# Expert rows weighted by ScalarE on the way out of PSUM and added onto y by an accumulating gather

## The reference, cut to what matters

```python
_, ys = jax.lax.scan(step, h0, xs)            # h = clip(bar_A * h + bar_B * x), y = sum(h * C) + x * D
ssm_out = jnp.swapaxes(ys, 0, 1)
flat = ssm_out.reshape(-1, d)
routing = jax.nn.softmax(flat @ Wr + br, axis=1)
top1_w = jnp.max(routing, axis=1)
top1_i = jnp.argmax(routing, axis=1)
hid = jax.nn.silu(jnp.einsum('nd,edf->enf', flat, up_w) + up_b[:, None, :])
all_out = jnp.einsum('enf,efd->end', hid, down_w) + down_b[:, None, :]
sel = jnp.take_along_axis(jnp.swapaxes(all_out, 0, 1), top1_i[:, None, None], axis=1)[:, 0, :]
moe_out = (sel * top1_w[:, None]).reshape(Bb, Ll, d)
out = ssm_out + moe_out
mu = jnp.mean(out, axis=-1, keepdims=True)
var = jnp.mean((out - mu) ** 2, axis=-1, keepdims=True)
return (out - mu) * jax.lax.rsqrt(var + EPS) * ln_w + ln_b
```

## Time and profile before

| | |
|---|---|
| median of 3 runs | 930.92 us (927.97 to 935.09) |
| the profiled execution | 928.69 us, its span 926.9 us |
| granted clock of PE, mean | 0.826 of full |
| indirect DMAs | 64 scatters, 64 gathers |
| weightings (L1080) | 64 |

### The profile page before, as it was taken

The page is one execution under the profiler, slowest core; times in us unless marked ns, Lnnn a source line. Parts: engine busy times, 40 slices in busy tenths (PEclk is TensorE's granted clock), DMA queues, the critical chain, the costliest instruction groups (busy, mean ns, idle before and its releaser), DMA issues.

```text
span 926.9 us, 14132 instructions
## 1 busy us (share of the span) xinstructions
PE 636.4 (69%) x4238; PEld 511.0 (55%) x4296; DVE 717.1 (77%) x1458; ACT 536.8 (58%) x988; POOL 565.2 (61%) x452
## 2 busy tenths in 40 slices
PE   3466658783799568964898289946985589358454
PEld 1244436671687448853777178825874388247333
DVE  3699898789979998799879997999879976431251
ACT  5373274664886659583958487647853484155222
POOL 0366547567874887478757876588648853541431
PEclk8566776996899779995999599967997599669766
DMA  3333445764367536663675447653665266316200
GB/s 101 117 136 114 137 141 166 257 215 166 115 229 244 199 110 202 210 179 115 209 252 166 159 138 258 210 185 114 217 220 189 84 215 199 114 56 197 74 7 23
DMA packets 82087, 149.31 MB, mean 161 GB/s; under 512 B 9404, under 2 KB 51144, under 8 KB 81992
## 3 DMA queue, kind: packets, MB, share of 16 engines
q1 hardware_dynamic: 69192, 135.13, 44.8%
q0 software_dynamic: 4096, 8.40, 2.8%
q10 hardware_dynamic: 8704, 4.72, 1.8%
HBM read 132.80 MB, written 15.40 MB: 160 GB/s over the span
## 4 chain that ended last, share of the span: by engine, by line
PE 30%; DVE 23%; ACT 17%; issue 16%; POOL 6%; DMA 5%; SPq 1%; ACTq 1%; another core or an unknown queue 0%; DVEq 0%; POOLq 0%
DVE state L1163 9%; PE psU L649 5%; ACT hid L800 4%; PE psD L552 4%; PE psT L663 4%; DVE psB L1154 3%; DMA weights<-in_w_pack 3%; PE psU L688 3%; PE psY L528 3%; ACT decay L761 3%; PE psU L689 2%; ACT x L820 2%; DVE bst L1097 2%; PE psU L577 1%; PE psB L522 1%
## 5 line engine op out<-in xcount | busy, mean ns | idle before, releaser
L1190 POOL TENSOR_TENSOR prod<-state,c_wide 128x1024 f32<-128x1024 f32 x128 | 308.8, 2419 | 151.7 <-DVE state L1163 132.1
L1154 DVE TENSOR_TENSOR psB<-dx,psB 128x512 f32<-128x512 f32 x256 | 166.7, 689 | 27.9 <-PE psB L522 12.1
L1163 DVE TENSOR_TENSOR_SCAN state<-decay,state,psB 128x512 f32<-128x512 f32 x128 | 163.8, 1280 | 14.0
L522 PE MATMUL psB<-parts,sel 128*128 128x512 bf16 x198 | 89.2, 464 | 122.7 <-DVE state L1163 121.0
L1163 DVE TENSOR_TENSOR_SCAN state<-decay,psB 128x512 f32<-128x512 f32 x128 | 155.1, 1212 | 3.8 <-ACT decay L761 3.8
L528 PE MATMUL psY<-ident,prod 128*128 128x128 f32 x1024 | 156.8, 308 | 0.7 <-POOL prod L1190 0.5
L761 ACT ACTIVATE decay<-delta,a_sb 128x1024 f32<-128x1024 f32 x128 | 142.0, 1142 | 15.1 <-DVE state L1163 7.3
L528 PEld LDWEIGHTS psY<-ident,prod 128*128 128x128 f32 x1024 | 139.2, 161 | 12.5 <-issue 8.1
L522 PEld LDWEIGHTS psB<-parts,sel 128*128 128x128 bf16 x256 | 25.8, 103 | 176.1 <-DVE state L1163 166.0
L800 ACT ACTIVATE hid<-psU,weights 128x128 f32<-128x128 f32 x352 | 99.3, 370 | 37.8 <-PE psU L649 32.5
L649 PE MATMUL psU<-yT_sorted,weights 128*128 128x128 f32 x704 | 95.5, 280 | 19.3 <-DVE hh L1134 8.0
(11 more groups left out here) (151 smaller groups left out, 1110.8 us busy)
## 6 DMA issues: line engine op xcount, KB each, us to landing
c_wide<-c_rows SPq DMA_DIRECT2D x128, 512.0 KB
weights<-in_w_pack SPq DMA_DIRECT2D x88, 514.0 KB, 4.1
xT_sb<-in_xT SPq DMA_DIRECT2D x8, 512.0 KB, 4.2
y_sorted<-rows_in SPq DMA_DIRECT2D x16, 256.0 KB, 3.1
xt<-in_x SPq DMA_DIRECT2D x8, 512.0 KB, 4.2
rows_out<-result SPq DMA_DIRECT2D x16, 256.0 KB, 4.3
out<-x ACTq DMA_DIRECT2D x16, 256.0 KB, 2.7
y_sorted<-rows_in SPq DMA_DIRECT2D x8, 192.0 KB, 3.9
```

Of the source, the lines that this page charges most:

```text
L522: pe.matmul(tokens(psB, c, h), sel[:, s, :], parts[:, c.n % 2, h * HALF:h * HALF + c.hw], start=True, stop=True).then_inc(b_ready, 1)
L1154: v.tensor_tensor(tokens(psB, c, h), dx[:, n % 2, h * HALF:h * HALF + c.hw], tokens(psB, c, h), ALU.mult).then_inc(inp_ready, 1)
L1163: v.tensor_tensor_scan(state[:, g % NSTATE, t0:t0 + c.hw], decay[:, g % NDECAY, t0:t0 + c.hw], tokens(psB, c, h), before, ALU.mult, ALU.ad ...
L1190: g_.tensor_tensor(prod[:, g % NPROD, w], state[:, g % NSTATE, w], c_wide[:, g % NC, w], ALU.mult).then_inc(prod_ready, 1)
```

## The change

The weight of a token travels with its row. ytok, y_sorted and rows_in get a 129th column. `router_pick` writes the weight into that column of ytok, so it has to run before `scatter` 0, which now waits for it; in the lists it stands in front of `slots`, and `router_exp` in front of decay 3. The scatter moves 129 numbers a row. `result` reads the weight from y_sorted as the scale of an Identity, so the rows that are stored are weighted already; `rows` now waits for all results of the chunk before. The gather no longer fills chosen_out: it is an indirect DMA that adds onto ytok (`compute_op=ALU.add`). `combine`, its semaphores, chosen_out and top_w are gone; `stats` h, 0 and `centre` read ytok, and `stats` h, 0 waits for the gathers. `y_copy` waits for `centre` of the chunk two before. rows_in is zeroed at the start in another shape. The five lists are written anew. The transposes out of ytok and y_sorted and the biases at the start take columns 0 to 127 (not shown). Of the five lists the new entries up to the marks are shown; `combine` stood in front of `scan` 4 and behind `scan` 7 on DVE, `x_shift` 1 between `prod` 4 and `gather` 5 on POOL.

```diff
 PE_ORDER = [
+    (0, "spread", 2, 0), (0, "spread", 2, 1), (0, "skip"), (-1, "logits"), (0, "spread", 3, 0), (0, "add", 0),
+    (0, "spread", 3, 1), (-1, "rank"), (0, "add", 1), (0, "spread", 4, 0), (0, "spread", 4, 1), (1, "bc"),
+    (0, "spread", 5, 0), (0, "spread", 5, 1), (0, "add", 2), (0, "add", 3), (0, "spread", 6, 0), (0, "spread", 6, 1),
+    (0, "spread", 7, 0), (0, "spread", 7, 1), (-2, "x_turn", 0), (-2, "x_rest", 0), (0, "add", 4),
+    (-2, "ff_up", 0, 0), (0, "spread", 8, 0), (-2, "ff_up", 0, 1), (0, "spread", 8, 1), (-2, "ff_up", 0, 2),
+    (0, "add", 5), (-2, "ff_up", 0, 3), (-2, "ff_up", 0, 4), (1, "b_turn"), (0, "spread", 9, 0), (0, "spread", 9, 1),
+    (-2, "ff_up", 0, 5), (-1, "sort_turn", 0), (0, "add", 6), (-1, "up", 0), (-1, "up", 1), (0, "spread", 10, 0),
+    (-1, "sort_turn", 1), (0, "spread", 10, 1), (-1, "down", 0), (-1, "up", 2), (-1, "down", 1), (0, "add", 7),
+    (0, "spread", 11, 0), (0, "spread", 11, 1), (-1, "down", 2), (-1, "sort_turn", 2), (-1, "up", 3),
+    (1, "b_spread", 0), (-2, "ff_down", 0), (0, "add", 8), (-2, "ff_part", 0, 0), (-2, "ff_part", 0, 1),
...
 ACT_ORDER = [
+    (-2, "silu", 8), (-2, "result", 8), (-2, "silu", 9), (-2, "silu", 10), (-2, "result", 9), (0, "decay", 0),
+    (-2, "result", 10), (-3, "norm", 1, 2), (0, "decay", 1), (-1, "y_copy"), (0, "decay", 2), (-1, "yT_copy"),
+    (1, "z_copy"), (-1, "router_exp"), (0, "decay", 3), (0, "decay", 4), (0, "decay", 5), (1, "softplus"),
+    (0, "decay", 6), (1, "bc_copy"), (0, "decay", 7), (-2, "norm", 0, 1), (0, "decay", 8), (-2, "x_high", 0),
...
 DVE_ORDER = [
+    (-2, "ff_mul", 0, 0), (-2, "ff_mul", 0, 1), (1, "b_max"), (-2, "ff_mul", 0, 2), (0, "scan", 9), (0, "scan", 10),
+    (1, "bc_low"), (-2, "affine", 1), (-2, "stats", 1, 1), (0, "scan", 11), (1, "bound", 0), (-2, "stats", 0, 2),
+    (0, "scan", 12), (0, "scan", 13), (1, "dx"), (1, "bound", 1), (-2, "ff_mul", 1, 0), (1, "over"),
+    (-2, "ff_mul", 1, 1), (-2, "ff_mul", 1, 2), (0, "scan", 14), (1, "flag"), (-2, "stats", 1, 2), (0, "scan", 15),
+    (1, "scan", 0), (1, "scan", 1), (1, "scan", 2), (0, "router_shift"), (1, "scan", 3), (0, "router_pick"),
+    (0, "slots"), (-1, "stats", 0, 0), (1, "scan", 4), (-1, "centre", 0), (1, "scan", 5), (1, "scan", 6),
+    (-1, "affine", 0), (-1, "stats", 0, 1), (2, "delta"), (1, "scan", 7), (-1, "stats", 1, 0), (-1, "centre", 1),
+    (1, "scan", 8),
 POOL_ORDER = [
+    (-1, "prod", 15), (-2, "x_shift", 1), (0, "prod", 0), (-2, "gather", 0), (0, "prod", 1), (-2, "gather", 1),
+    (-2, "gather", 2), (-2, "gather", 3), (0, "prod", 2), (0, "prod", 3), (-2, "gather", 4), (-2, "gather", 5),
+    (-2, "gather", 6), (-1, "scatter", 0), (-1, "scatter", 1), (-2, "rstd", 0, 0), (-1, "scatter", 2), (0, "prod", 4),
+    (-2, "gather", 7), (-1, "scatter", 3), (-2, "rstd", 0, 1), (-1, "scatter", 4), (-1, "scatter", 5),
+    (-1, "scatter", 6), (-1, "scatter", 7), (0, "prod", 5), (0, "prod", 6), (1, "bc_rest"), (0, "prod", 7),
+    (0, "prod", 8), (-2, "rstd", 1, 0), (0, "prod", 9), (1, "bound_input"), (-2, "rstd", 1, 1), (0, "prod", 10),
+    (-2, "rstd", 0, 2), (0, "prod", 11), (-1, "x_shift", 0), (0, "prod", 12), (0, "prod", 13), (0, "prod", 14),
+    (-2, "rstd", 1, 2),
 SP_ORDER = [
+    (-2, "c", 5), (-3, "weights", 1), (-3, "weights", 2), (-2, "c", 6), (-2, "c", 7), (-3, "rows"), (-2, "c", 8),
+    (-2, "c", 9), (-2, "c", 10), (-3, "weights", 3), (-2, "c", 11), (-3, "weights", 4), (-3, "weights", 5), (-3, "x"),
+    (-2, "c", 12), (-3, "weights", 6), (-2, "c", 13), (-3, "weights", 7), (-3, "weights", 8), (-3, "weights", 9),
+    (-1, "over"), (-2, "c", 14), (-3, "weights", 10), (-2, "c", 15), (-1, "c", 0), (-3, "store", 0), (0, "xT"),
+    (-1, "c", 1), (-3, "store", 1), (-3, "store", 2), (-1, "c", 2), (-1, "c", 3), (-2, "weights", 0), (-1, "c", 4),
@@ -293,11 +292,10 @@
         c_wide = sb("c_wide", [D, NC, L])
         prod = sb("prod", [D, NPROD, L])
 
-        ytok = sb("ytok", [128, 2, 2 * NJ, D])
+        ytok = sb("ytok", [128, 2, 2 * NJ, D + 1])
         rs = sb("rs", [128, 2 * NJ, E])
         ex = sb("ex", [128, 2 * NJ, E])
         rsmall = sb("rsmall", [128, 3, 2 * NJ])
-        top_w = sb("top_w", [128, 2, 2 * NJ])
         rcode = sb("rcode", [128, 2 * NJ, E])
         chosen = sb("chosen", [128, 2 * NJ, E], BF16)
         over_size = sb("over_size", [128, E, L // ROWS])
@@ -455,6 +451,7 @@
                 if name == "rows":
                     sp_.wait_ge(scattered, 16 * (c.tiles0 + c.tiles))
                     wait(sp_, turned, c.groups0)
+                    wait(sp_, result_ready, c.blocks0)
                     for g, (k0, k1) in enumerate(c.groups):
                         sp_.dma_start(y_sorted[:, k0:k1, :], rows_in.rearrange("(k p) d -> p k d", p=ROWS)[:, k0:k1, :]
                                       ).then_inc(sorted_in[g], 16)
@@ -765,9 +763,9 @@
                     for h in range(2):
                         if n > 1:
                             p = CHUNKS[n - 2]
-                            wait(act, mixed[h], p.with_half[h] + (p.halves > h))
+                            wait(act, centred[h], p.with_half[h] + (p.halves > h))
                     for h in range(c.halves):
-                        ins = nc.scalar.activation(ytok[:, n % 2, h * NJ:h * NJ + c.hj, :], psY[:, h * NJ:h * NJ + c.hj, :],
+                        ins = nc.scalar.activation(ytok[:, n % 2, h * NJ:h * NJ + c.hj, 0:D], psY[:, h * NJ:h * NJ + c.hj, :],
                                                    ACT.Copy)
                     ins.then_inc(y_copied, 1)
                 if name == "yT_copy":
@@ -805,7 +803,8 @@
                     (d,) = banks_of(c, ("down", k))
                     act.wait_ge(filled[d], fills(d, c, ("down", k)))
                     wait(act, stored, 16 * c.groups0)
-                    nc.scalar.activation(result[:, k, :], bank[d][:, 0:D], ACT.Copy).then_inc(drained[d], 1)
+                    nc.scalar.activation(result[:, k, :], bank[d][:, 0:D], ACT.Identity, scale=y_sorted[:, k, D:D + 1]
+                                         ).then_inc(drained[d], 1)
                     act.wait_ge(drained[d], fills(d, c, ("down", k)))
                     act.sem_inc(result_ready, 1)
                 if name == "norm":
@@ -1028,7 +1027,7 @@
                     dve.wait_ge(router_exp, n + 1)
                     v.tensor_reduce(rsmall[:, 2, j], ex[:, j, :], X, ALU.add).then_inc(router_steps, 1)
                     dve.wait_ge(router_steps, 7 * n + 6)
-                    v.reciprocal(top_w[:, n % 2, j], rsmall[:, 2, j]).then_inc(router_steps, 1)
+                    v.reciprocal(ytok[:, n % 2, j, D], rsmall[:, 2, j]).then_inc(router_steps, 1)
                 if name == "slots":
                     m = c.tiles * E
                     t = bank["T"]
@@ -1070,22 +1069,11 @@
                     dve.wait_ge(blocks_ready, 2 * n + 2)
                     dve.wait_ge(slots_ready, n + 1)
                     v.memset(first_block[:, 0:1], 0.0).then_inc(drained["T"], 1)
-                if name == "combine":
-                    (h,) = args
-                    dve.wait_ge(gathered[h], 16 * NJ * (c.with_half[h] + 1))
-                    dve.wait_ge(router_steps, 7 * (n + 1))
-                    wait(dve, affined[h], c.with_half[h])
-                    for j in range(c.hj):
-                        jj = h * NJ + j
-                        ins = v.scalar_tensor_tensor(out=moe[:, jj, :], in0=chosen_out[:, jj, :],
-                                                     scalar=top_w[:, n % 2, jj:jj + 1], in1=ytok[:, n % 2, jj, :],
-                                                     op0=ALU.mult, op1=ALU.add)
-                    ins.then_inc(mixed[h], 1)
                 if name == "stats":
                     h, k = args
                     turn = c.with_half[h]
                     if k == 0:
-                        dve.wait_ge(mixed[h], turn + 1)
+                        dve.wait_ge(gathered[h], 16 * NJ * (turn + 1))
                     elif k == 1:
                         dve.wait_ge(affined[h], turn + 1)
                     else:
@@ -1093,7 +1081,7 @@
                     wait(dve, rstd_ready[h], 3 * turn + k)
                     for j in range(c.hj):
                         jj = h * NJ + j
-                        src = (moe[:, jj, :], attn[:, jj, :], bank["D"][:, j * 128:(j + 1) * 128])[k]
+                        src = (ytok[:, n % 2, jj, 0:D], attn[:, jj, :], bank["D"][:, j * 128:(j + 1) * 128])[k]
                         ins = v.bn_stats(bst[:, h, j, :], src)
                     ins.then_inc(stats_local, 1)
                     dve.wait_ge(stats_local, 1)
@@ -1109,7 +1097,7 @@
                     dve.wait_ge(stats_steps[h], 3 * turn + 1)
                     for j in range(c.hj):
                         jj = h * NJ + j
-                        ins = v.scalar_tensor_tensor(out=moe[:, jj, :], in0=moe[:, jj, :], scalar=mv[:, h, j, 0:1],
```

(10 more changed lines are left out.)

88 lines of the change are left out of this document (27 added, 61 removed), and 3 rows, old and new, of the table SP_ORDER.

## The result

| | before | after |
|---|---|---|
| median, us (20 runs each) | 929.2 (925.7 to 935.1) | 932.4 (928.6 to 938.9) |
| ratio | | 1.0034, 95% interval 1.0018 to 1.0049 |
| profiled execution, us (span) | 928.7 (926.9) | 928.6 (926.8) |

The account below looks back on a forecast made before the run. DVE was taken to bound each period up to 448 us, then PE. Six periods of -2.6 + 0.3 (-13.8), tail -4.6, last chunk -1.5 make -19.9 us: 908.8 profiled, 911 us median; own range 901 to 918, over the cases 898 to 932.

Parts of the forecast that it names:

- The accumulating gather: On POOL: priced at +0.1 us over a plain gather's 0.98 us, between bounds of 0 and 0.98; nothing a period.
- rival C: POOL's accumulating gather costs half as much again, 0.49 us more; 7.5 us saved in all, 923 us; chance 0.13.
- the 0.65: Added us per accumulating gather from which its cost a period, 8x - 2.4, eats the 2.6 us gained.
- its own 0.3 us for ScalarE: `result` with a pointer as scale: some 100 ns, 11 times a period, a third on the path, +0.3 us a period.
- the text's own formula: POOL: x us more per gather lengthens a period by (4x - 0.9) + (4x - 1.5) us, each bracket only where positive.
- the 1.65 us up to scan 8: Scan 8 starts at 437.3 us, held by POOL's product 5, so 1.65 of DVE's 3.8 us arrive each period.
- time taken from DVE before 448 us is on the path: First half of a period: DVE's freed time shortens the path until POOL or PE takes over; 2.6 us a period taken.
- rival B: PE's half gives nothing back, the 2.6 us are waited away; tail and last chunk leave 925 us; chance 0.12.
- the 1.5 us forecast for the last chunk: Last chunk: weighting of 1.89 us leaves the chain, 0.4 us go back for four dearer gathers: -1.5 us.
- the 4.6 us forecast there: Chunk 6's tail: `x_shift` and two gathers move ahead of the scatters into waited time; `shift` near 811.6 us, -4.6 us.
- the wait for product 5 ahead of scan 8: Sign: DVE waits some 2 us for POOL's product 5 ahead of scan 8.
- the vanished wait of scan 10: All three `ff_mul` stand ahead of scan 9, so DVE's 0.93 us wait for PE in scan 10 goes, each period.

Follow-up runs that it names:

- run 5: Changed kernel with its eight gathers a period in eight forms (plain or accumulating, 128 or 64 rows or columns, strided or dense); ran once, 920.8 us.
- run 2: Kernel before with its gathers accumulating onto the buffer they used to write over, old lists and weighting kept: 953.1 us, ratio 1.024.
- run 1: Changed kernel with its eight gathers a period made plain, the addition of y left out, new lists kept: 920.8 us, ratio 0.989.
- run 3: Kernel before without DVE's weighting and addition of y, gathers writing the statistics' input directly, old lists: 925.7 us, ratio 0.995.
- run 6: Changed kernel with product 5 directly behind the root on POOL's list: 933.5 us; also spread 8 earlier on PE's: 937.3; first edit with plain gathers: 922.2.
- run 7: Changed kernel with scatters 1 and 2 behind product 4 on POOL's list, so product 4 ends before the affine of half 0: 932.2 us, ratio 1.003.
- run 10: Changed kernel with ScalarE's result as a plain copy, the weighting by the router's probability left out: 930.0 us, ratio 1.001.
- run 4: Computation of the kernel before (plain gathers, weighting by DVE) in the changed kernel's five lists: 963.8 us, ratio 1.036.

## Why the prediction was wrong

Forecast and result lie 21.4 us apart; in the two stretches of the profiled executions it is -19.9 forecast and +1.5 measured. Three parts make it: a price taken too low, freed time taken as worth too much, and the end.

**The accumulating gather (11.5 us).** "I take +0.1, since it is one instruction nearest to the plain gather." It measured +0.60 us, inside the bounds of 0 and 0.98 and near rival C's 0.49, and just short of the 0.65 from which the text let the loss begin (with its own 0.3 us for ScalarE a period loses from x = 0.59). What rival C took from the Trainium skill (Collectives: The Full Stack, section The bandwidth ceiling: the fold count and why AG ≠ RS ≠ AR), an added read descriptor for each piece, no run shows: the packets of a gather rise from 32 to 144, not by half, and in run 5 POOL's time does not go by rows, so that C's 0.49 is near for another reason. The value between two far ends should not have been taken next to the lower one on the strength of "one instruction": the one fact at hand, a second source to be read, spoke for the middle.

With x = 0.6 the text's own formula gives 1.5 + 0.9 us for a period and 0.1 us in sum, where -0.2 was measured. That is luck: in the new lists, for which the formula was counted, the accumulation costs 0.85 and not 2.4, and the freed time brings less, too. In the old lists 2.4 is near (2.8 in run 2).

**What DVE's time is worth (7.4 us in the periods).** Forecast were 2.6 - 0.3 us a period; with plain gathers 1.07 came. The step that failed is the 1.65 us up to scan 8: run 1 has 0.5. POOL's count was right up to the root (23.2 us behind the router against 23.6), then the root took 2.7 us in place of 1.9, its first operation 1.09 us beside DVE's two-input work, and scan 8 started 0.6 us after product 5's end, for which the sum had nothing. Behind it lies a larger mistake: the sentence "time taken from DVE before 448 us is on the path". DVE's busy 41.97 of 44 us didn't say that. The second weighting (3.17 us) stood beside a chain as long as itself, statistics, root, norm, turn, up projections; run 3 took it out, and 2.3 us of wait for PE took its place. The 925.7 us of run 3 meet rival B's 925 us by luck: B had PE's half give nothing back and 6.1 us come from the end, while run 3 has PE late in both halves and 1.4 us from the end. That the chain holds scan 8 is shown by runs 3, 6 and 7; that it sets the whole period is argued only.

**The end (2.5 us).** Forecast -6.1; with plain gathers it was -3.6, with accumulating ones +2.8. There nothing covers POOL. The last chunk after, POOL, then DVE:

```profile
867.57 1.64 POOL L1206 DMA_INDIRECT ytok<-rows_out,slot  x1 [4.61 <-DMA rows_out<-result]
...
878.78 1.69 POOL L1206 DMA_INDIRECT ytok<-rows_out,slot  x1 [0.30 <-issue]
879.92 0.79 POOL L1215 TENSOR_TENSOR ve<-mv,eps 128x4 f32<-128x4 f32 x1
```

```profile
876.49 0.87 DVE L1085 BATCH_NORM_STATS2 bst<-ytok 128x6 f32<-128x128 f32 x4 [16.64 <-DMA ytok<-rows_out,slot]
...
882.01 1.14 DVE L1114 SCALAR_TENSOR_TENSOR attn<-moe,rstd,xt 128x128 f32<-128x128 f32 x4 [2.96 <-issue]
```

The first gather starts 79.6 us behind the last y copy, as before (870.47 us there), and the affine 94.1 us behind it where before had 91.0 (881.91): the root stands behind seven gathers on POOL's list, 4.2 us dearer, and the text counted four, 0.4 us dearer. With plain gathers the way from first gather to affine is 10.3 us against 11.4 before, so there 1.2 of the 1.5 us forecast for the last chunk come. Ahead of chunk 6's scatters there are seven more; they end at 800.87 us, 3.4 us behind the slots they could start with. So also of the 4.6 us forecast there (816.0 - 811.6 is 4.4) only 1.1 came, counted from the last y copy to `shift` (24.0 us against 25.1), and 2.8 with plain gathers (22.3 us).

**Right were** the wait for product 5 ahead of scan 8 in kind (3.81 us, two forecast), the vanished wait of scan 10, DVE's busy time (24.8 us down for 22), `result` at 366 ns (370), ScalarE's term as far as run 10 can tell (2.4 us between medians, 1.8 forecast), that no `stats` waits for a gather outside the end, and that `router_exp` delays no scan. The stall did move, to the affine and not to `centre`; run 7 shows that it cost nothing there, within the 1 us the text allowed. The Trainium skill's rule of the shared port pair (SBUF — State Buffer, section SBUF: two separate sides) is borne out by that stall (1.7 us) and by the 10.61 us of run 4.

## What to carry over

Ask of freed time on a busy engine what else ends where that time ends: a chain over other engines as long as the freed work makes it nearly worthless, however full the engine looks. Moving work to shorten such a chain can cost more than it gives: look first at what the moved operations will fall on. An operation that no row shows and that moves work to the fullest queue deserves a run of its own before it is priced. And price it by stretch: the same gathers cost 0.85 us a period in one order, 2.8 in another, and 6.3 us once in the uncovered end, where the plain form and an addition on the idle DVE make the best complete kernel measured.

## What was not expected of the hardware

- An accumulating indirect gather occupies POOL 1.58 us against 0.98 us, nearly independent of rows and columns (1.44 us for 64 rows), lands in 3.3 us (after) against 3.0 (run 1), and makes 144 packets for 32 (11264 less 64 scatters of 32, over 64 gathers; with plain gathers run 1 has 4096 for both).
- In run 4 four DVE operations with two SBUF inputs, of 0.34 us each elsewhere, took 10.61 us while POOL ran four operations without a gap; the longest single one of the run took 9.84 us. It is no slowing in proportion: DVE stood until POOL's row of work ended.
- It goes the other way too: in run 1 POOL's small addition ahead of the root took 1.09 us (424.71) beside DVE's `delta`, also of two SBUF inputs (424.55 to 425.74 us), and 0.2 us elsewhere.
